# A two-layer transformer on one Trainium2 core: the second attention's products and heads in one block, with 80 maxima beside the products

## The chip, the core and the metric

The kernel runs on one core of a Trainium2 chip. Five engines work side by side, each with its own instruction list, and wait for one another through semaphores: TensorE (PE in the profile; PEld are its weight loads), VectorE (DVE), ScalarE (ACT), GpSimd (POOL) and SyncE (SP), which here only issues DMA transfers. SBUF is the on-chip memory of 128 partitions; PSUM holds TensorE's results in eight banks of 512 float32 per partition. The metric is the time of one execution on the device in microseconds. Three runs of the kernel before took 1679.89, 1681.15 and 1681.57 us: median 1681.15 us.

## The reference, cut to what matters

1024 tokens of 512 features pass four sublayers, each as `x = x + layernorm(f(layernorm(x)))`: a latent attention, a gated feed-forward layer (inner width 1792), a second attention with 32 heads of 16 features, and a linear layer with dequantized weights. The change is about the third:

```
qkv = x @ attn_qkvw + attn_qkvb                  # 1024 x 1536
q, k, v = split into 32 heads of hd = 16
scores = einsum('bhqd,bhkd->bhqk', q, k) * scale
probs = softmax(scores)
ctx = einsum('bhqk,bhkd->bhqd', probs, v)
out = ctx @ attn_ow + attn_ob
```

## The kernel before, in words

Everything is float32 in effect. Where an exact product is wanted, each operand is split into an upper part that TensorE takes at full rate and a lower part (the rest), and three matmuls (upper-upper, upper-lower, lower-upper) are summed.

A block is a piece of program with one instruction list for each engine; the next block begins when all engines have ended the last one. The stages around the change are these:

1. **Norm block `n2`** (`norm_block`). For each of eight token tiles of 128 TensorE makes the feed-forward's down projection (42 matmuls), VectorE and ScalarE normalize it, add it to `x`, normalize again, TensorE transposes the result and ScalarE and VectorE write it as `h_hi` and `h_lo`. The transposes of tile t stand behind the projection of tile t + 1, those of the last tile behind everything.
2. **Inputs block** (`mha_inputs`). SyncE fetches the weights of queries, keys and values (1 MB each); ScalarE and VectorE split each whole (128 x 2048). TensorE then makes 16 products for queries and keys (feature block of 128 by half the tokens) and 8 for values (a token tile each), 12 matmuls each. For queries and keys ScalarE adds the bias into `full`, VectorE casts the upper part and subtracts the lower, and SyncE stores both in DRAM (`qk_scratch`, 256 KB each). Values go to DRAM too (`v_scratch`), 32 columns per head: 16 values and 16 ones, so that mixing also gives the sums of the softmax.
3. **Heads block** (`mha_heads`). Eight groups of four heads. A group's *stacks* hold, on 48 partitions per head, query and key parts one above the other (three rows of 16), so that one matmul gives the exact score; a 49th row holds the negative maximum (queries) or ones (keys). Twelve transfers of 128 KB build the stacks of a group from `qk_scratch`, three stack buffers rotate.
   - *Maxima.* For the softmax's maximum TensorE makes each score tile once (128 queries x 512 keys) into `ah_ring`, three PSUM banks in turn, and VectorE reduces it to one column: 64 per group, 512 in all. After 32 of them VectorE joins and transposes them, and SyncE writes them as row 49 of the query stack.
   - *Units.* A unit is 128 keys by 512 queries for the four heads. TensorE makes two pairs of scores, ScalarE two exponentials over 1024 columns, TensorE mixes them with the values (eight rows of the trace) into `ah_mix`. 16 units per group, 128 in all. After eight units ScalarE copies out the result and SyncE, VectorE and GpSimd divide it by the sums.
   - *Order.* `maxima_before(n, stage)` says how many maxima TensorE has issued before which part of unit n. 56 stand alone before unit 0, then four stand in each unit until all 512 are issued with unit 114; the last 14 units have none.
   - SyncE issues all transfers in one written order: the first three groups' stacks and values ahead, later groups' stacks in two halves of six between the small transfers of each half group.
4. **Tail block** (`mha_tail`). Output projection, norm, linear layer, norm.

## Time and profile before

| | us |
|---|---|
| median of three runs | 1681.15 |
| profiled execution, its own time | 1682.93 |
| its span, first to last instruction | 1680.7 |
| TensorE busy | 1528.2 (91%) |
| VectorE busy | 1039.1 (62%) |
| ScalarE busy | 809.2 (48%) |
| GpSimd busy | 227.9 (14%) |

The profile comes from one execution; its span is 2.2 us shorter than that execution's own time. Rows of the view by windows give, for each stretch, its length and then each engine's busy time with the number of instructions, TensorE's granted clock as a share of full speed (1.00 is 2.4 GHz, 0.50 is 1.2 GHz), the busy share of the 16 DMA engines and what they moved. Rows of the timeline give start, duration, engine, source line, operation, what is written and read, shapes and count, and in brackets how long the engine had been idle and what released it. Rows of a source line give the shortest, middle and longest duration in ns. Records of neighbouring instructions on one engine can overlap, so a pace is read from starts. Busy shares over the whole span say little here: stages with different limits follow one another.

### The profile page before, as it was taken

Reading aid. Unit: us, or ns where it says so; the run is one execution under the profiler, and the core shown is the slowest. Engines: PE = TensorE matmul, PEld = TensorE weight load, DVE = VectorE, ACT = ScalarE, POOL = GpSimd, SP = SyncE. Lnnn points to the kernel's source line nnn. Section 1 sums busy time; section 2 is a strip of 40 time slices with the busy share of each in tenths; the row PEclk is TensorE's granted clock in tenths of the full one; section 3 lists DMA queues with packets and bytes.
Section 4 is the critical chain, followed back from the end, with each engine's and each line's share of the span. In section 5 each row is a group of like instructions: output and inputs, shape, how many; then the busy total and the mean of one; then the engine's idle time right before and its main releaser. Section 6 shows DMA issues by size and latency. Waiting matters only on the chain. (4 is left out here: it accounts for less than half of the span.)

```text
span 1680.7 us, 22663 instructions
## 1 busy us (share of the span) xinstructions
PE 1528.2 (91%) x8286; PEld 1004.9 (60%) x8286; DVE 1039.1 (62%) x1801; ACT 809.2 (48%) x1458; POOL 227.9 (14%) x225
## 2 busy tenths in 40 slices
PE   6867999999999999969989998969599999999987
PEld 4645666666777666748768887848443333333254
DVE  5744666666666666625543443644199999999345
ACT  4325666666666666522122212213017777777834
POOL 2752111111111121000000000000000033331200
PEclk9977999999999999989979999989859999999999
DMA  4142212212221221153211111024670334431001
GB/s 132 55 180 69 88 61 67 66 62 67 94 67 60 67 67 39 32 182 99 88 63 57 61 53 50 1 82 176 170 106 8 76 78 87 88 71 35 18 13 44
DMA packets 71714, 125.23 MB, mean 75 GB/s; under 512 B 13054, under 2 KB 38782, under 8 KB 70318
## 3 DMA queue, kind: packets, MB, share of 16 engines
q1 hardware_dynamic: 71540, 123.67, 25.4%
q8 instruction: 67, 1.10, 0.3%
q14 instruction: 43, 0.35, 0.1%
q0 software_dynamic: 64, 0.11, 0.0%
HBM read 87.23 MB, written 33.85 MB: 72 GB/s over the span
## 5 line engine op out<-in xcount | busy, mean ns | idle before, releaser
L1641 DVE TENSOR_REDUCE ah_minus_half<-ah_ring 128x1 f32<-128x512 f32 x512 | 317.5, 679 | 35.3 <-PE ah_ring L1569 35.3
L958 DVE TENSOR_REDUCE mh_minus_max<-mh_score 128x1 f32<-128x128 f32 (+7 forms) x256 | 193.7, 757 | 196.2 <-PE mh_score L772 196.0
L1624 ACT ACTIVATE ah_probs<-ah_score 128x1024 f32<-128x1024 f32 x256 | 247.8, 1022 | 134.6 <-PE ah_score L1584 134.0
L1569 PE MATMUL ah_ring<-ah_k_stack,ah_q_stack 48*128 48x512 f32 x512 | 203.8, 491 | 34.8 <-DMA ah_k_stack<-qk_scratch 18.9
L1569 PEld LDWEIGHTS ah_ring<-ah_k_stack,ah_q_stack 48*128 48x128 f32 x512 | 92.3, 197 | 210.0 <-DVE ah_minus_half L1641 184.2
L882 ACT ACTIVATE mh_probs<-mh_score,mh_minus_max 128x128 f32<-128x128 f32 (+7 forms) x256 | 189.9, 742 | 35.7 <-DVE mh_minus_max L958 33.3
L1584 PE MATMUL ah_score<-ah_q_stack,ah_k_stack 49*128 49x512 f32 x512 | 154.2, 434 | 1.7 <-ACT ah_probs L1624 1.7
L768 PE MATMUL mh_score<-shared,h_hi 128*128 128x512 f32 (+3 forms) x384 | 151.6, 395 | 2.7 <-ACT mh_probs L882 2.7
L1031 POOL TENSOR_TENSOR h_lo<-mh_pe,h_hi 64x512 fp32r<-64x512 f32 x64 | 81.8, 1278 | 470.0 <-ACT h_hi L868 466.4
L1599 PE MATMUL ah_mix<-ah_probs,ah_v 128*32 128x512 f32 x1024 | 137.2, 608 | 0.6 <-ACT ah_probs L1624 0.6
L769 PE MATMUL mh_score<-shared,h_hi 128*128 128x512 f32 (+3 forms) x384 | 131.9, 344 | 0.0
L770 PE MATMUL mh_score<-shared,h_lo 128*128 128x512 f32 (+3 forms) x384 | 131.8, 343 | 0.0
L782 PE MATMUL mh_turn<-ident,mh_probs 128*128 128x128 f32 x672 | 107.5, 277 | 2.5 <-DVE mh_high_turned L967 0.4
L768 PEld LDWEIGHTS mh_score<-shared,h_hi 128*128 128x128 f32 x384 | 73.1, 190 | 60.0 <-ACT mh_probs L882 36.5
L892 ACT COPY mh_high_turned<-mh_turn 128x128 f32<-128x128 f32 (+3 forms) x128 | 54.6, 426 | 105.0 <-PE mh_turn L787 105.0
L808 PE MATMUL mh_mix<-mh_high_turned,ck 128*64 128x512 f32 (+3 forms) x512 | 102.8, 524 | 0.0
L967 DVE COPY mh_high_turned<-mh_turn 128x512 f32<-128x512 f32 x128 | 87.5, 684 | 4.6 <-PE mh_turn L782 3.4
L1584 PEld LDWEIGHTS ah_score<-ah_q_stack,ah_k_stack 49*128 49x128 f32 x512 | 79.6, 187 | 17.9 <-ACT ah_probs L1624 15.3
L787 PE MATMUL mh_turn<-ident,mh_probs 128*128 128x128 f32 x480 | 84.4, 274 | 0.0
L1204 DVE TENSOR_TENSOR d<-x,ff_up 128x512 f32<-128x512 f32 x28 | 19.3, 688 | 102.7 <-PE ff_up L1157 102.7
L1178 ACT ACTIVATE x<-ff_gate 128x512 f32<-128x512 f32 x28 | 16.7, 598 | 136.8 <-PE ff_gate L1157 136.8
L770 PEld LDWEIGHTS mh_score<-shared,h_lo 128*128 128x128 f32 x384 | 73.0, 190 | 7.0
(224 smaller groups left out, 2892.9 us busy)
## 6 DMA issues: line engine op xcount, KB each, us to landing
mh_w<-in_w_pairs SPq DMA_DIRECT2D x16, 896.0 KB, 5.6
x<-in_w_inner SPq DMA_DIRECT2D x14, 768.0 KB, 4.1
pe_scratch<-fr_pe_out SPq DMA_DIRECT2D x4, 2048.0 KB, 6.6
mh_pe<-pe_scratch SPq DMA_DIRECT2D x16, 512.0 KB, 4.0
mh_spread<-inverse_scratch SPq DMA_DIRECT2D x64, 128.0 KB, 2.9
a_scratch<-mh_mixed SPq DMA_DIRECT2D x32, 256.0 KB, 2.3
x<-a_scratch SPq DMA_DIRECT2D x8, 1024.0 KB, 5.7
qk_scratch<-shared SPq DMA_DIRECT2D x32, 256.0 KB, 2.0
```

The costliest lines, as they stand in the source:

```text
L768: nc.tensor.matmul(out, q_hi[:, i % 2, e, q], m["kt_hi"][e][:, k], start=True, stop=False)
L769: nc.tensor.matmul(out, q_hi[:, i % 2, e, q], m["kt_lo"][e][:, k], start=False, stop=False)
L770: last = nc.tensor.matmul(out, q_lo[:, i % 2, e, q], m["kt_hi"][e][:, k], start=False, stop=not diagonal)
L782: last = nc.tensor.transpose(turn_ps[0][:, j, :], probs[:, s % 2, j * P:(j + 1) * P], ident[:])
L808: last = nc.tensor.matmul(mix_ps[e * CR:(e + 1) * CR, q0:BANK], m["ck"][:, j, 0:CR], high_turned[:, j, e, q0:BANK], start=j == 0, stop=j = ...
L882: nc.scalar.activation(probs[:, s % 2, 0:width], score_ps[s % 2][:, base:base + width], ACT.Exp, bias=minus_max[:, s % 4:s % 4 + 1], accum ...
L958: nc.vector.reduce_max(minus_max[:, s % 4:s % 4 + 1], score_ps[s % 2][:, base:base + width], AX.X, negate=True).then_inc(max_ready, 1)
L1569: return nc.tensor.matmul(ring[:, m % 3, :], q_stack[a][stack_rows(p, PARTS), c, t * P:(t + 1) * P], k_stack[a][stack_rows(p, PARTS), c, h ...
L1584: last = nc.tensor.matmul(score_ps[c][:, p, :], k_stack[a][rows, c, j * P:(j + 1) * P], q_stack[a][rows, c, half * BANK:(half + 1) * BANK] ...
L1599: last = nc.tensor.matmul(mix_ps[rows, :], v[a][:, j, rows], probs[:, 2 * (u % 2) + c, p * BANK:(p + 1) * BANK], start=j == 0, stop=j == N ...
L1624: nc.scalar.activation(probs[:, 2 * (u % 2) + c, :], score_ps[c][:].rearrange("p e n -> p (e n)"), ACT.Exp, scale=MHA_SCALE).then_inc(prob ...
L1641: nc.vector.reduce_max(minus_half[:, m:m + 1], ring[:, m % 3, :], AX.X, negate=True).then_inc(max_taken, 1)
```

## The change

The inputs block is gone. A class `Products` holds its work, spread over the two blocks beside it:

- In the norm block SyncE fetches the weights when the operand `d`, on whose place they go, has been split. ScalarE and VectorE split the first two pieces (128 columns of the key and of the query weights) while tile 6 is in work; TensorE makes products 0 and 1, which need only the first half of the tokens, between the last projection and the last transposes.
- In the heads block products 2 to 23 come first. Their order is now key and query of the same feature block in turn, so that groups 0 and 1 can be loaded after products 0 to 3. Their PSUM banks are those of the scores. From product 8 on there are five maxima beside each product, two behind its first six matmuls and three behind the rest: 80 before unit 0. The other 432 are spread over units 0 to 113, 3.79 per unit.
- ScalarE writes the upper part straight from PSUM, VectorE the lower part straight from PSUM with one instruction; the weights are split in pieces of 128 x 512.
- Values stay in SBUF (eight tensors, ones written by GpSimd); `v_scratch` and its transfers go.
- Group 0's stacks are issued half by SyncE, half by ScalarE; groups 1 and 2 by SyncE beside the stores; groups 3 to 7 by ScalarE, one transfer behind the second exponential of units 1 to 12 of a group.
- Many tensors of the later stages lie at fixed places inside `d`, `down_hi`, `down_lo`, `shared` and `h`.

The diff, cut to its core:

```diff
+                if following is not None:
+                    following.load(sp)
...
+            if following is not None:
+                pe.wait_ge(ht_used, NT // 2)
+                for n in range(2):
+                    following.product(pe, n, range(ND))
...
+                if following is not None and t == NT - 2:
+                    following.upper(act, 0)
+                    following.upper(act, 1)
...
-def mha_inputs(nc, io, h, spare, w_hi, w_lo, hi, lo, scratch):
...
+    def piece(self, i):
+        if i < 2 * ND:
+            c, cols = 1 - i % 2, slice(i // 2 * P, (i // 2 + 1) * P)
+            return tuple(m[c][:, :, cols] for m in (self.w, self.w_hi, self.w_lo))
+        return tuple(m[2][:, i - 2 * ND, :] for m in (self.w, self.w_hi, self.w_lo))
...
+    def product(self, pe, n, steps):
+        if steps[0] == 0:
+            wait(pe, self.lo_ready, min(n - 3, self.NQK))
+            wait(pe, self.v_ready, n - 3 - self.NQK)
+            pe.wait_ge(self.w_ready, n // 4 * 2 + 1 + n % 2 if n < self.NQK else 2 * ND + ND)
...
+    def take_upper(self, act, n):
+        kind, blk, _ = self.place(n)
+        if n == 0:
+            act.wait_ge(self.bias_in, 32)
+        act.wait_ge(self.ready, n + 1)
+        if n >= 4:
+            act.wait_ge(self.part_out[n % 4], 32 * (n // 4))
+        row = kind * ND + blk
+        self.nc.scalar.activation(self.ring[:, n % 4, 0, :], self.bank(n), ACT.Identity, bias=self.bias_qk[:, row:row + 1]
+                                  ).then_inc(self.hi_ready, 1)
...
+    def take_lower(self, dve, n):
+        kind, blk, _ = self.place(n)
+        row = kind * ND + blk
+        dve.wait_ge(self.hi_ready, n + 1)
+        self.nc.vector.scalar_tensor_tensor(self.ring[:, n % 4, 1, :], self.bank(n), self.bias_qk[:, row:row + 1],
+                                            self.ring[:, n % 4, 0, :].bitcast(F32), ALU.add, ALU.subtract).then_inc(self.lo_ready, 1)
...
-        PER_UNIT = NMAX // NUNIT
-        LEAD = 6 * PER_UNIT
-        FIRST = HALF_MAX + LEAD
+        FROM = 8
+        FIRST = 5 * (products.COUNT - FROM)
+        AHEAD = 6
...
+        def maxima_at(unit):
+
+            return min(FIRST - (-unit * (TOTAL - FIRST) // (UNITS - NT - AHEAD)), TOTAL)
...
+        def maxima_beside(n, part):
+
+            return max(5 * (n - FROM) + (2, 5)[part], 0)
...
-            def load_stacks(g, row_halves):
-                a = g % DEPTH
-                wait(sp, scores_ready, 2 * NUNIT * (g - DEPTH + 1))
...
-            def load_v(g):
-                a = g % DEPTH
-                wait(sp, mixed, NUNIT * (g - DEPTH + 1))
-                sp.dma_start(v[a][:], v_rows[:, :, 4 * g * 2 * HD:4 * (g + 1) * 2 * HD]).then_inc(v_in[a], 16)
...
-                load(g)
+            for n in range(4):
+                products.store(sp, n, scratch["qk"])
+            for n in range(4):
+                sp.wait_ge(products.part_out[n], 32)
+            load_stacks(sp, 0, (0,))
+            for n in range(4, products.NQK):
+                products.store(sp, n, scratch["qk"])
+                if n in (5, 7):
+                    load_stacks(sp, 1, (n // 2 - 2,))
             put_max(0, 0)
+            for n in range(4):
+                sp.wait_ge(products.part_out[n], 32 * products.NQK // 4)
             put_ones(2)
-            load(2)
+            load_stacks(sp, 2, range(2))
             put_max(0, 1)
             sp.dma_start(bias_f[:], io["biases"]).then_inc(later_in, 16)
...
-                if DEPTH <= g + 2 < GROUPS:
-                    load_stacks(g + 2, (0,))
...
+                if (g, u, c) == (0, 0, 0):
+                    pe.wait_ge(products.v_ready, NT)
...
+            for n in range(2, products.COUNT):
+                for part in range(2):
+                    products.product(pe, n, range(2 * part, 2 * part + 2))
+                    while done < maxima_beside(n, part):
+                        one_maximum(done)
+                        done += 1
...
+            pieces = {1: (2, 3), 3: (4, 5), 7: (6, 7), 8: (8,), 9: (9,), 10: (10,), 11: (11,)}
+            for n in range(products.NQK):
+                products.take_upper(act, n)
+                for i in pieces.get(n, ()):
+                    products.upper(act, i)
+                if n == 3:
+                    for i in range(4):
+                        act.wait_ge(products.part_out[i], 32)
+                    load_stacks(act, 0, (1,))
...
+            def load_one(g, n):
+                a = g % DEPTH
+                if n == 0:
+                    act.wait_ge(scores_ready, 2 * NUNIT * (g - DEPTH + 1))
+                p, kind, n, part = stack_loads[n]
+                stack = (q_stack, k_stack)[kind][a]
+                act.dma_start(stack[64 * p + n * HD:64 * p + (n + 1) * HD, :, :].bitcast(F32),
+                              qk_rows[part, kind, g, p]).then_inc(stacks_in[a], 16)
...
+                    if 1 <= u <= STACK_DMAS and DEPTH <= g + 2 < GROUPS:
+                        load_one(g + 2, u - 1)
...
+            for n in range(products.COUNT + 1):
+                if n < products.NQK:
+                    products.take_lower(dve, n)
+                elif n < products.COUNT:
+                    take_value(n)
+                for i in pieces.get(n, ()):
+                    products.lower(dve, i)
+                until = maxima_beside(n + 1, 1) if n + 1 < products.COUNT else FIRST if n < products.COUNT else TOTAL
+                while m < until:
...
+                    if inverted < NHALF * GROUPS and maxima_at(NT * (inverted + 1) + AHEAD) < min(m + 1, TOTAL):
+                        shares.invert(dve, inverted)
```

Where instructions move, the order of the instruction lists shows it. The first place is TensorE at the end of the norm block. Before: `n_py` is the down projection, `n_pt` the transposes, `ai_ps` the first product.

```order
L1900 MATMUL n_py<-down_lo,shared 128x512
L1900 MATMUL n_py<-down_hi,shared 128x512
L126 MATMUL n_pt<-ident,n_hn 128x128 x8
L87 UNCONDITIONAL_BRANCH
L1265 UNCONDITIONAL_BRANCH
L1281 MATMUL ai_ps<-h_hi,down_hi 128x512
L1281 MATMUL ai_ps<-h_lo,down_hi 128x512
```

Now (`ah_score` holds the products, `ai_w` are the weights' parts; the 24 matmuls of two products are cut to their first and last):

```order
L1963 MATMUL n_py<-down_lo,shared 128x512
L1963 MATMUL n_py<-down_hi,shared 128x512
L128 MATMUL n_pt<-ident,n_hn 128x128 x4
L1309 MATMUL ah_score<-h_hi,ai_w_hi_11230 128x512
L1309 MATMUL ah_score<-h_lo,ai_w_hi_11230 128x512
...
L1309 MATMUL ah_score<-h_hi,ai_w_lo_11232 128x512
L128 MATMUL n_pt<-ident,n_hn 128x128 x4
L87 UNCONDITIONAL_BRANCH
L1572 UNCONDITIONAL_BRANCH
L1309 MATMUL ah_score<-h_hi,ai_w_hi_11230 128x512
```

The last four transposes stand behind two products, and the third product follows the one block border that is left.

The second place is VectorE from the last products to the maxima. Before: `shared` is the lower part of a query or key product, `d` a value product, `ah_minus_half` a reduced maximum, `ah_rows` the turned maxima.

```order
L1318 TENSOR_TENSOR shared<-d,shared 128x512
L1325 TENSOR_TENSOR d<-ai_ps,ai_bias_v 128x32x16 x8
L1225 UNCONDITIONAL_BRANCH
L1637 UNCONDITIONAL_BRANCH
L1663 MEMSET ah_minus_max 128x32 x2
L1641 TENSOR_REDUCE ah_minus_half<-ah_ring 128x1 x34
L1650 TENSOR_TENSOR ah_minus_max<-ah_minus_half 128x4x2x2
L1641 TENSOR_REDUCE ah_minus_half<-ah_ring 128x1
L1659 STREAM_TRANSPOSE ah_rows<-ah_minus_max 32x32 x4
```

Now, from product 9 on:

```order
L1294 TENSOR_TENSOR ai_w_lo_11234<-ai_w_11228,ai_w_hi_11231 128x512
L1683 TENSOR_REDUCE ah_minus_half<-ah_ring 128x1 x5
L1328 SCALAR_TENSOR_TENSOR ai_ring<-ah_score,ai_bias_qk,ai_ring 128x512
L1294 TENSOR_TENSOR ai_w_lo_11234<-ai_w_11228,ai_w_hi_11231 128x512
L1683 TENSOR_REDUCE ah_minus_half<-ah_ring 128x1 x5
...
L1328 SCALAR_TENSOR_TENSOR ai_ring<-ah_score,ai_bias_qk,ai_ring 128x512
L1683 TENSOR_REDUCE ah_minus_half<-ah_ring 128x1 x4
L1692 TENSOR_TENSOR ah_minus_max<-ah_minus_half 128x4x2x2
```

The reductions stand five by five between the lower parts of the products (and, up to product 11, a piece of weights), instead of in one run behind all of them.

The third place is ScalarE around the units. Before: `ah_probs` are exponentials, `ah_out` the copied result.

```order
L1298 ACTIVATE d<-ai_ps,ai_bias_qk 128x512 x13
L1225 UNCONDITIONAL_BRANCH
L1614 UNCONDITIONAL_BRANCH
L1624 ACT_TABLE_LOAD
L1624 ACTIVATE ah_probs<-ah_score 128x1024 x18
L1619 COPY ah_out<-ah_mix 128x512
```

Now, from the last products to the first units of group 1:

```order
L1321 ACTIVATE ai_ring<-ah_score,ai_bias_qk 128x512 x4
L1643 ACT_TABLE_LOAD
L1643 ACTIVATE ah_probs<-ah_score 128x1024 x18
L1638 COPY ah_out<-ah_mix 128x512
L1643 ACTIVATE ah_probs<-ah_score 128x1024 x16
L1638 COPY ah_out<-ah_mix 128x512
L1643 ACTIVATE ah_probs<-ah_score 128x1024 x2
L1664 DMA ah_q_stack_11958<-qk_scratch 16x2x1024
L1643 ACTIVATE ah_probs<-ah_score 128x1024 x2
L1664 DMA ah_q_stack_11958<-qk_scratch 16x2x1024
```

From group 1 on, a transfer of the stacks stands behind each pair of exponentials, twelve times in a group's sixteen units.

## Rows read from the trace of the kernel before

**Rows 1.** Windows: length, engines' busy us (x instructions), PEclk, DMA share, GB/s.

```profile
1114.40:1122.10 7.70, 1.54 (x8) 0.91 (x6) 5.42 (x11) 1.69 (x4) 0.00 (x0) 0.83 0.00 0
1122.10:1132.20 10.10, 0.01 (x1) 0.01 (x1) 3.26 (x3) 1.90 (x1) 0.00 (x0) 0.50 0.85 299
1132.20:1199.80 67.60, 67.59 (x288) 55.47 (x288) 27.17 (x41) 14.64 (x18) 0.00 (x0) 0.97 0.48 184
1199.80:1218.60 18.80, 0.00 (x0) 0.00 (x0) 0.82 (x3) 1.28 (x1) 0.20 (x1) 0.63 0.83 133
1218.60:1252.10 33.50, 32.57 (x55) 15.28 (x55) 32.59 (x59) 0.00 (x0) 0.00 (x0) 0.50 0.65 98
1252.10:1569.70 317.60, 302.53 (x1822) 115.34 (x1821) 296.59 (x542) 229.50 (x243) 69.36 (x69) 0.99 0.32 63
1569.70:1598.70 29.00, 26.69 (x173) 7.20 (x172) 1.87 (x8) 26.84 (x29) 6.32 (x6) 1.00 0.07 18
1598.70:1680.70 82.00, 63.02 (x244) 44.37 (x240) 44.28 (x122) 31.27 (x58) 3.17 (x3) 0.91 0.08 30
```

**Rows 2.** Timeline: start, us, engine, line, operation, operands, [idle before <- releaser].

```profile
1100.41 2.03 DVE L1893 TENSOR_TENSOR shared<-d,shared 128x1792 fp32r<-128x1792 f32 x1 [0.84 <-ACT shared L1889]
1119.62 1.12 PE L126 MATMUL n_pt<-ident,n_hn 128*128 128x128 f32 x4 [4.79 <-DVE n_hn L204]
1132.19 0.80 PE L1281 MATMUL ai_ps<-h_hi,down_hi 128*128 128x512 f32 x1 [11.46 <-DVE down_lo L1305]
1193.06 0.39 PE L1281 MATMUL ai_ps<-down_hi,h_lo 128*128 128x512 f32 x1
...
1199.40 0.39 PE L1281 MATMUL ai_ps<-down_lo,h_hi 128*128 128x512 f32 x1
1218.64 1.22 PE L1569 MATMUL ah_ring<-ah_k_stack,ah_q_stack 48*128 48x512 f32 x3 [18.85 <-DMA ah_k_stack<-qk_scratch]
```

**Rows 3.** Windows, while the first stacks are fetched.

```profile
1206.00:1218.00 12.00, 0.00 (x0) 0.00 (x0) 0.00 (x0) 0.00 (x0) 0.00 (x0) 0.50 1.05 127
```

**Rows 4.** Timeline of TensorE, two units, one with a join.

```profile
1352.28 0.49 PE L1569 MATMUL ah_ring<-ah_k_stack,ah_q_stack 48*128 48x512 f32 x1 [0.57 <-DVE ah_minus_half L1641]
1352.70 1.06 PE L1599 MATMUL ah_mix<-ah_probs,ah_v 128*32 128x512 f32 x8
1353.70 0.50 PE L1569 MATMUL ah_ring<-ah_k_stack,ah_q_stack 48*128 48x512 f32 x1
...
1355.40 1.06 PE L1599 MATMUL ah_mix<-ah_probs,ah_v 128*32 128x512 f32 x8
```

**Rows 5.** Timeline of VectorE (lone maxima) and of ScalarE (a unit).

```profile
1219.47 20.42 DVE L1641 TENSOR_REDUCE ah_minus_half<-ah_ring 128x1 f32<-128x512 f32 x34 [15.30 <-PE ah_ring L1569]
...
1357.16 1.94 ACT L1624 ACTIVATE ah_probs<-ah_score 128x1024 f32<-128x1024 f32 x2 [0.76 <-PE ah_score L1584]
```

**Rows 6.** Groups by line: busy us, mean ns of one, idle before.

```profile
L1641 DVE TENSOR_REDUCE ah_minus_half<-ah_ring 128x1 f32<-128x512 f32 x512 | 317.5, 679 | 35.3 <-PE ah_ring L1569 35.3
L1318 DVE TENSOR_TENSOR shared<-d,shared 128x512 fp32r<-128x512 f32 x16 | 11.1, 693 | 0.6
L1298 ACT ACTIVATE d<-ai_ps,ai_bias_qk 128x512 f32<-128x512 f32 x16 | 11.0, 690 | 34.3 <-PE ai_ps L1281 34.3
L1325 DVE TENSOR_TENSOR d<-ai_ps,ai_bias_v 128x512 f32<-128x512 f32 x8 | 5.5, 692 | 15.0 <-PE ai_ps L1281 15.0
L943 DVE SCALAR_TENSOR_TENSOR w_vo_lo<-mh_prep,kw,w_vo_hi 128x512 fp32r<-128x512 f32 x16 | 11.9, 743 | 3.7 <-ACT w_vo_hi L856 3.7
```

**Rows 7.** SyncE's issues: timeline, source line (ns), stores' landing, issues by operand.

```profile
1204.19 1.34 SPq L1451 DMA_DIRECT2D ah_q_stack<-qk_scratch  x3
L1451 SPq DMA_DIRECT2D ah_q_stack<-qk_scratch x48: 321/424/1082, 1204.2 to 1509.9; - x48
DMA to landing us min/median/max: 2.0/2.0/3.7
mh_spread<-inverse_scratch SPq DMA_DIRECT2D x64, 128.0 KB, 2.9
```

298 lines of the change are left out of this document (146 added, 152 removed).

## The prediction, made before the changed kernel had run

> **What bounds the kernel now.** I read the span in stretches first [rows 1]. It ends in one line of stages, each of which waits for the one before, so a stretch in which no engine works at its limit is paid in full. From the end of the second norm block to the last mixing product there are seven: 7.7 us in which TensorE works 1.5, 10.1 us without any (0.01), 67.6 us of query, key and value products with TensorE at 67.59, 18.8 us without any, 33.5 us of maxima alone, 317.6 us of units with maxima, and 29.0 us of the last 14 units.
>
> The timeline of TensorE says what ends the gaps [rows 2]: the last transposes wait 4.79 us for VectorE's normed tile, the first product 11.46 us for the split weights, the first maximum 18.85 us for the stacks. With full clock a product matmul comes every (1199.40 - 1193.06)/28 = 0.2264 us, so 288 take 65.2 us; the stretch lasted 67.6 because the clock was low in its first 4 us. The clock column [rows 1] shows 0.83 in the norm's last stretch, with its pause of nearly 5 us, 0.50 in the gap before the products, 0.50 again while the stacks are fetched and in the whole stretch of lone maxima.
>
> In a unit [rows 4] mixing takes 1353.70 - 1352.70 = 1.00 us and four maxima and four scores 1355.40 - 1353.70 = 1.70 us, 0.2125 each: 2.70 us, TensorE without a pause. Once every eight units VectorE joins and turns its maxima, and TensorE waits 0.57 us for a free slot of the ring of three; that unit takes 0.50 us more. 114 x 2.70 + 14 x 0.50 = 314.8 of 317.6 us; the other 2.8 us are the first two units, begun at low clock. VectorE takes 34 reductions in 20.42 us, 0.60 apart (one is recorded with 0.68 [rows 6], so they overlap), and ScalarE's two exponentials take 1.94 us of a unit [rows 5].
>
> **Part 1: weights and two products inside the norm block.** The weights are fetched as soon as the operand `d` is split, and split in ScalarE's and VectorE's pauses. The first two products, 24 x 0.2264 = 5.4 us, stand in the 4.79 us pause, so the last transposes come some 0.6 us later, but at full clock (they took 1.12 us at low). The block therefore ends where it did, at 1122.1 to 1122.3, and product 2 begins at about 1122.7. The other 22 products take 22 x 2.717 = 59.8 us. Without maxima they would end at 1182.5 instead of 1199.8.
>
> **Part 2: stacks and maxima beside the products.** Maxima begin in the middle of product 8, at 1122.7 + 6 x 2.72 + 1.36 = 1140.4 if the stacks are there. They are not: product 3 ends at 1128.4, its two parts (0.69 on ScalarE, 0.74 on VectorE [rows 6]) at 1129.9, and its store, issued in 0.3 us, lands 2.0 us later (2.0 to 3.7 [rows 7]), so 1132.1. Before, the twelve transfers of the first group took from 1204.19 [rows 7] to 1218.64 [rows 2] = 14.4 us. I take the same: 1146.5, a pause of 6 us on TensorE. Bounds: 9 us if twelve ran with nothing beside them and overlapped their start (1141), 20 us if the eight stores and six more transfers behind them take their share of the engines first (1152). I choose 14.4 because the DMA share was already 1.05 in those 12 us at 127 GB/s [rows 3]: the transfers themselves were the limit, not their issue.
> The Trainium skill, "DMA: Bandwidth & Descriptors", "Issuing engines are not separate DMA queues", says that transfers started by several engines share the same 16 DMA engines and that only issue time is saved. By that rule half of the stacks on ScalarE's queue gains nothing over 14.4 us; if the two queues added up, the stacks would land near 1139.5 and the sum would be 5 us better. The row of share 1.05 sides with the rule.
>
> From the first maximum on VectorE is the later one: 80 reductions x 0.60 = 48.1; 8 lower parts of queries and keys by a form that reads PSUM, a bias and the upper part, 0.74 each by the same form elsewhere plus 0.03 between instructions = 6.2; 8 values x 0.72 = 5.8; 4 pieces of value weights x 0.72 = 2.9; two joins with their transposes 2.0. That is 65.0 us, against 15.5 x 2.72 + 80 x 0.213 = 59.2 on TensorE. With a ring of three the two can't run far apart; I add 2.3 us for the handovers (the last value waits for its product) and get the first score at 1146.5 + 67.3 = 1213.8. Before it was 1252.1: **-38.3 us**. If the lower part takes 0.69, as the plain subtraction does [rows 6], that is 0.4 us less. The pause of 6 us will let the clock fall for some us, as nearly 5 us did in the norm, but VectorE is the limit behind it, so I price that at nothing; with TensorE as the limit it is 2.4 us, as in the product stretch (67.6 - 65.2).
>
> Hidden at no cost: the removed stores and loads of values, the cast on VectorE, GpSimd's eight memsets (it is idle there [rows 1]), the later load of the exponential's table, which falls into ScalarE's wait for the last value.
>
> **Part 3: the units.** 432 maxima over the same 114 units instead of 456: 24 x 0.2125 = 5.1 us less. A join moves in front of the units (-0.5) and the first units run at full clock (-2.8). **-8.4 us**. VectorE's load falls with the maxima, so nothing takes their place; in units with three maxima TensorE needs 2.49 us and ScalarE 1.94.
>
> **Part 4: later stacks issued by ScalarE.** Sixty units now have one transfer behind their second exponential. Its issue took 0.42 us on SyncE in the middle of 96, from 0.31 to 1.08 [rows 7]. ScalarE has 2.65 - 1.94 = 0.71 us to spare in a mean unit, so up to about 0.7 us is free: I take 0.42 and no cost; the upper bound 1.08 costs 60 x 0.37 = 22 us; the lower, nothing. No row shows an issue on ScalarE. What does come late: group 3's first maximum is number 192, in unit 29, and its last transfer is issued behind the exponentials of unit 28, 2.0 us after unit 28's first score is done, and lands 2.9 us later (128 KB from DRAM, issue to landing [rows 7]), 4.9. TensorE reaches that maximum at 2.70 + 4 x 0.2125 = 3.6: **+1.3 us** once, 0.4 if it lands in 2.0 like a store, 3.1 if the engines are busy and it takes 4.7. Later groups have more room, as the maxima run ahead less.
>
> What is queued behind the new waits: SyncE's stores of products 4 to 7 stand behind six transfers of group 0 and twelve of group 1. ScalarE writes ring slot n mod 4 only when the store of product n - 4 has landed, and VectorE's maxima stand behind that. By 127 GB/s group 0 and the first half of group 1 are done near 1153, store 6 by 1154; product 10 ends at 1157. Room of 3 us.
>
> **The sum.** -38.3 - 8.4 + 1.3 = -45.4 us. The 29.0 us of the last units (1.94 us of exponentials in 2.07) and the 82.0 us behind [rows 1] stay. Span 1680.7 - 45.4 = 1635.3; the profiled execution, 2.2 us more than its span (1682.93), would be 1637.5; the median of the runs, 1681.15, is 1.8 under it and becomes 1635.7. I say 1636.
>
> **Rivals.**
> ScalarE's issue is dear. Against it: 0.42 median; for it: it stands in line between exponentials, and no row shows it there. At 1.08 each: 1636 + 22 = 1658.
> Stores and stacks collide. 6 MB (24 stack transfers of 128 KB, 12 stores of 256 KB) want the DMA engines within 30 us, at a share of 1.05 for the stacks alone. If the stacks land at 1152 and one slot of the ring waits 4 us: 1646.
> The first stacks are early. ScalarE and SyncE issue in parallel, nothing else moves at first; at 1141 it is 5.5 us less: 1631.
> Slower than before: the same 60 issues, if each holds ScalarE for more than 0.7 + 45/60 = 1.45 us, since the exponentials then set the unit. At 1.6 us they cost 60 x 0.89 = 53 us: 1689. For it: only that a transfer on a busy queue may hold its issuer (1.08 at most on SyncE, with 12 in a row). Against it: it is one transfer per unit, 128 KB in 2.7 us, where the engines move that in 1.0.
> The change doing less than it says: if the products waited for the weights inside the norm, it would show before the last transposes. In the norm's last stretch the DMA share is 0.00 [rows 1], so the fetch finds free engines; it can start when the operand's last split ends, at 1102.4 [rows 2], its first 512 KB are needed on ScalarE at about 1109 and at 299 GB/s take 1.7 us. It gets no number of its own.
>
> **Chances.** Forecast 0.65 (its own range 1630 to 1643); collision 0.14; early stacks 0.09; dear issue 0.08; slower 0.04. The range 1627 to 1653 holds the first three and leaves out most of the last two. About 0.2% (3.4 us) can be told apart by measurement: faster 0.95, within it 0.01, slower 0.04.
>
> **What will show it.** Right: no 11 us wait before the first product; a wait of about 6 us on the stacks' transfers in the middle of product 8, maxima from 1146 on; first exponential near 1214; product cadence 4.4 to 4.5 us for products 8 to 11, then 3.85; units of 2.70 and, every fifth or so, 2.49; ScalarE's issues near 0.42 and no wait of scores for exponentials beyond before's. One wait of 1 to 2 us at unit 29. Wrong: units over 2.7 us where a transfer is issued; VectorE idle in the product stretch while ScalarE waits for a store.

## The result and the profile after

The changed kernel takes 1636.05 us, the median of four runs (1633.25 to 1639.19); before, beside it, 1680.52 us (1679.36 to 1681.57). The ratio is 0.9736, with a 95% interval of 0.9713 to 0.9759. Predicted were 1636 us. One execution, the profiled one of (4) with 1677.60 us, lies more than 1.5% above the fastest of its kernel and is left out of the medians and ratios.

The profiled execution is the shortest of the four: 1633.25 us, span 1631.4, so it lies 2.8 us under the median. The columns are those of [rows 1].

```profile
1114.40:1120.80 6.40, 4.75 (x23) 3.73 (x23) 4.36 (x8) 0.88 (x2) 0.03 (x1) 1.00 0.00 0
1120.80:1143.90 23.10, 17.96 (x78) 14.55 (x78) 9.45 (x16) 8.26 (x14) 4.40 (x9) 0.95 0.80 182
1143.90:1216.70 72.80, 70.34 (x266) 41.89 (x266) 63.48 (x110) 8.81 (x13) 0.39 (x2) 0.97 0.54 124
1216.70:1240.00 23.30, 22.86 (x124) 9.68 (x125) 19.40 (x36) 15.72 (x16) 0.00 (x0) 0.85 0.00 1
1240.00:1549.00 309.00, 297.21 (x1844) 109.91 (x1843) 262.12 (x482) 241.10 (x255) 75.19 (x73) 1.00 0.21 54
1554.40:1631.40 77.00, 62.44 (x240) 44.18 (x240) 44.00 (x122) 30.68 (x57) 3.21 (x3) 0.92 0.08 30
```

The stretches without TensorE (10.1 and 18.8 us) and the lone maxima (33.5 us) of [rows 1] are gone, and the norm's last stretch runs at clock 1.00 instead of 0.83. What answers to [rows 2] in TensorE's timeline:

```profile
1118.55 0.60 PE L128 MATMUL n_pt<-ident,n_hn 128*128 128x128 f32 x4
1120.82 0.47 PE L1309 MATMUL ah_score<-h_hi,ai_w_hi 128*128 128x512 f32 x1 [1.67 <-PEq L87]
...
1143.94 0.79 PE L1580 MATMUL ah_ring<-ah_k_stack,ah_q_stack 48*128 48x512 f32 x2 [5.17 <-DMA ah_k_stack<-qk_scratch]
...
1216.73 0.69 PE L1597 MATMUL ah_score<-ah_q_stack,ah_k_stack 49*128 49x512 f32 x2 [2.34 <-DVE ah_v L1707]
...
1296.65 0.46 PE L1580 MATMUL ah_ring<-ah_k_stack,ah_q_stack 48*128 48x512 f32 x1 [0.78 <-DMA ah_k_stack<-qk_scratch]
```

Before, TensorE waited 4.79, 11.46 and 18.85 us. Now 5.17 us on the first stacks are left, and two waits are new: 2.34 us before the first score and 0.78 us in a unit, on the stacks of group 3. The transfers issued by ScalarE and the stores, by source line (shortest, middle, longest; ns), against [rows 7]:

```profile
L1664 ACTq DMA_DIRECT2D ah_q_stack<-qk_scratch x30: 309/310/314, 1264.6 to 1455.6; - x30
...
L1664 ACTq DMA_DIRECT2D ah_k_stack<-qk_scratch x30: 309/310/330, 1272.1 to 1463.9; - x30
...
L1336 SPq DMA_DIRECT2D qk_scratch<-ai_ring x32: 319/320/640, 1121.9 to 1182.2; - x32
...
DMA to landing us min/median/max: 2.0/3.6/14.8
```

The span, cut at the same events in both traces, beside the terms of the prediction:

| stretch | before | predicted | after |
|---|---|---|---|
| first product of the heads block starts at | - | 1122.7 | 1120.82 |
| from it to the first maximum | - | 23.8 | 23.1 |
| first maximum to first score | - | 67.3 | 72.8 |
| first score at | 1252.1 | 1213.8 | 1216.73 |
| first score to first mixing | 4.9 | 4.9 | 4.4 |
| first to last mixing (127 units) | 340.7 | 333.6 | 327.8 |
| last mixing to the end | 83.0 | 83.0 | 82.5 |
| span | 1680.7 | 1635.3 | 1631.4 |

The total was right; two terms were not, with opposite signs: the stretch from the first maximum to the first score is 5.5 us longer than forecast, the units 5.8 us shorter. The experiments are about these two, about what each part of the change is worth, and about the spread of 6 us between executions.

### The profile page after: what moved, and what is told of

The parts are those of the page before. It is cut to its first block and busy times, and to the rows that moved or that the text cites. A ratio compares the mean times of both kernels' runs of the same rounds, so it can differ in the third digit from the quotient of the medians.

```text
span 1631.4 us, 22633 instructions
## 1 busy us (share of the span) xinstructions
PE 1512.2 (93%) x8286; PEld 990.9 (61%) x8286; DVE 1031.7 (63%) x1792; ACT 810.1 (50%) x1467; POOL 232.1 (14%) x233
## 5 line engine op out<-in xcount | busy, mean ns | idle before, releaser
L1580 PE MATMUL ah_ring<-ah_k_stack,ah_q_stack 48*128 48x512 f32 x512 | 184.3, 461 | 15.3 <-DMA ah_k_stack<-qk_scratch 5.9
L1580 PEld LDWEIGHTS ah_ring<-ah_k_stack,ah_q_stack 48*128 48x128 f32 x512 | 81.5, 187 | 176.2 <-DVE ah_minus_half L1683 160.4
L1597 PEld LDWEIGHTS ah_score<-ah_q_stack,ah_k_stack 49*128 49x128 f32 x512 | 76.0, 187 | 22.4 <-ACT ah_probs L1643 15.5
L1963 PE MATMUL n_py<-down_hi,shared 128*128 128x512 f32 x224 | 72.5, 400 | 4.9 <-DVE shared L1956 4.9
```

What stands on the lines that cost most here:

```text
L1580: return nc.tensor.matmul(ring[:, m % 3, :], q_stack[a][stack_rows(p, PARTS), c, t * P:(t + 1) * P], k_stack[a][stack_rows(p, PARTS), c, h ...
L1597: last = nc.tensor.matmul(score_ps[c][:, p, :], k_stack[a][rows, c, j * P:(j + 1) * P], q_stack[a][rows, c, half * BANK:(half + 1) * BANK] ...
```

## Experiments

Parts of the change were undone or altered one at a time, then the rules found were tested and used. Every ratio is against the kernel before, run on the same chip. The changed kernel itself ran on one chip only; the medians of the kernel before, taken beside each run, lie between 1679.24 and 1680.52 us, so 1.3 us of a difference between medians can be the chip's. "Block start" is the first product of the heads block.

**1. The two parts of the front.** First without maxima beside products, then with part 1 undone.

```diff
 def maxima_beside(n, part):
-    return max(5 * (n - FROM) + (2, 5)[part], 0)
+    return 0
```

> The changed kernel with its 80 first maxima in one run behind the products, as before, instead of five beside each product from product 8 on. In the changed kernel's profile product 2 begins at 1120.8, the first score stands at 1216.7. Main theory (a maximum beside a product costs about 0.31 us, since a product with five takes 4.28 us instead of 2.72, and one alone costs VectorE's 0.60): products end at 1120.8 + 22 x 2.72 = 1180.6, then 80 x 0.60 = 48 and two joins, first score near 1231; the clock falls beside the lone maxima, 2.8 us more in the first units. Time 1636 + 14 + 3 = 1653. Rival (placing them beside the products saves nothing that the pause for the stacks and the switching between product and maximum don't take back): 1636 to 1640.

Measured 1648.68 us (1644.86 to 1653.8), ratio 0.9819 (0.9795 to 0.9843): 12.6 us over the changed kernel. Windows, products and then lone maxima:

```profile
1118.60:1182.80 64.20, 60.64 (x264) 49.33 (x264) 22.61 (x35) 17.14 (x27) 4.41 (x9) 1.00 0.70 181
1182.80:1231.50 48.70, 46.40 (x81) 21.34 (x80) 48.45 (x89) 0.00 (x0) 0.39 (x2) 0.55 0.25 33
```

TensorE no longer waits for the stacks, which land while it makes products, but the 80 maxima then go at VectorE's pace (48.7/80 = 0.61 us each) with TensorE at clock 0.55. From block start to first score it takes 112.9 us against 95.9. Putting maxima beside products is worth 17 us of that stretch in the traces and 12.6 in the medians.

```diff
-        vector_work=vector_work, projected=used, following=products)
+        vector_work=vector_work, projected=used)
 # and in the heads block, ahead of everything:
+            products.load(sp)
...
-            for n in range(2, products.COUNT):
+            for n in range(products.COUNT):
...
+            products.upper(act, 0)
+            products.upper(act, 1)
...
+            products.lower(dve, 0)
+            products.lower(dve, 1)
```

> The changed kernel with the weights' fetch, the first two pieces and products 0 and 1 taken out of the norm block and put at the head of the heads block. Main theory (part 1 of the prediction): the fetch of the first 512 KB and one piece split by ScalarE and VectorE stand in front, 5 to 6 us; two products of 2.72 us more behind it; 2.4 us of low clock. Time 1636 + 13 = 1649, and the pause before the stacks stays as it is (about 5 us). Rival (the products are followed by a pause for the stacks, which counts from product 3, so nothing before it is hidden, but VectorE limits the rest, so low clock costs nothing): 1646. Rival (the norm block's end moved by as much as it gained): 1637.

Measured 1649.05 us (1644.9 to 1651.4), ratio 0.9814 (0.9794 to 0.9835). TensorE's timeline:

```profile
1127.42 0.79 PE L1309 MATMUL ah_score<-h_hi,ai_w_hi 128*128 128x512 f32 x1 [7.17 <-DVE ai_w_lo L1294]
...
1156.13 0.77 PE L1581 MATMUL ah_ring<-ah_k_stack,ah_q_stack 48*128 48x512 f32 x2 [2.99 <-DMA ah_k_stack<-qk_scratch]
```

The wait for the weights is back (7.17 us), and two products more stand behind it. Part 1 is worth 13.0 us, as this run's main theory had it (1649).

**2. Which engine sets the pace: VectorE's reductions made shorter.**

```diff
-nc.vector.reduce_max(minus_half[:, m:m + 1], ring[:, m % 3, :], AX.X, negate=True).then_inc(max_taken, 1)
+nc.vector.reduce_max(minus_half[:, m:m + 1], ring[:, m % 3, 0:256], AX.X, negate=True).then_inc(max_taken, 1)
```

> The changed kernel with each maximum's reduction over the first 256 of its 512 columns only (half of the columns is left out of the maxima). TensorE's work is unchanged; VectorE's 0.60 per maximum becomes about 0.33. Theory of the ring (in a unit with four maxima the fourth waits for the slot of the first, which is free 0.53 + 0.68 + 0.06 = 1.27 us after its matmul began; TensorE is not the limit): units fall from 2.70 to about 2.35, the product stretch by 3 to 4 us, the joins' 0.5 us go; time 1600 to 1606. Theory of the prediction (a unit is TensorE's 2.70 us without a pause): units stay at 2.70, only the joins' waits and the handovers beside the products go, 1628 to 1632.

Measured 1602.14 us (1597.74 to 1603.39), ratio 0.9535 (0.9519 to 0.9551). Two rows of VectorE beside value products of the changed kernel, then of this one:

```profile
1192.85 1.89 DVE L1683 TENSOR_REDUCE ah_minus_half<-ah_ring 128x1 f32<-128x512 f32 x3 [0.61 <-PE ah_ring L1580]
1194.65 0.68 DVE L1707 TENSOR_TENSOR ah_v<-ah_score,ai_bias_v 128x512 f32<-128x512 f32 x1
```

```profile
1187.18 1.09 DVE L1683 TENSOR_REDUCE ah_minus_half<-ah_ring 128x1 f32<-128x256 f32 x3 [1.28 <-PE ah_ring L1580]
1188.19 0.68 DVE L1707 TENSOR_TENSOR ah_v<-ah_score,ai_bias_v 128x512 f32<-128x512 f32 x1
1189.42 0.76 DVE L1683 TENSOR_REDUCE ah_minus_half<-ah_ring 128x1 f32<-128x256 f32 x2 [0.56 <-PE ah_ring L1580]
```

Beside value products the pace did not move: from the first value to the last, seven products, it is 29.88 us in the changed kernel (1186.11 to 1215.99) and 29.87 here (1179.65 to 1209.52), though VectorE is now idle 1.28 + 0.56 us in such a product. There VectorE was not the bound. It was the bound in two other places: products 9 to 12 take 4.25 to 4.29 us instead of 4.43 to 4.51, and product 15, beside which VectorE joins and turns the first maxima, 4.26 instead of 5.05. That is 1.6 of the 3.0 us by which this trace is shorter from first maximum to first score (69.8 against 72.8 us). In the units the pace did move: from first to last mixing it is 299.0 us instead of 327.8. TensorE's weight loads of a unit with four maxima, in the changed kernel and in this one, show why (a row is the load, so its start is the moment TensorE takes the matmul up):

```profile
1239.32 0.18 PEld L1580 LDWEIGHTS ah_ring<-ah_k_stack,ah_q_stack 48*128 48x128 f32 x1 [0.84 <-DVE ah_minus_half L1683]
1239.33 0.29 PEld L1597 LDWEIGHTS ah_score<-ah_q_stack,ah_k_stack 49*128 49x128 f32 x2
1239.43 0.44 PEld L1580 LDWEIGHTS ah_ring<-ah_k_stack,ah_q_stack 48*128 48x128 f32 x2
1239.70 0.39 PEld L1597 LDWEIGHTS ah_score<-ah_q_stack,ah_k_stack 49*128 49x128 f32 x2
1240.60 0.18 PEld L1580 LDWEIGHTS ah_ring<-ah_k_stack,ah_q_stack 48*128 48x128 f32 x1 [0.51 <-DVE ah_minus_half L1683]
1241.03 0.16 PEld L1612 LDWEIGHTS ah_mix<-ah_probs,ah_v 128*32 128x32 f32 x8 [0.25 <-issue]
```

VectorE's row of the same unit, and then the loads of the kernel with half reductions:

```profile
1239.86 2.48 DVE L1683 TENSOR_REDUCE ah_minus_half<-ah_ring 128x1 f32<-128x512 f32 x4 [0.22 <-PE ah_ring L1580]
```

```profile
1354.30 0.18 PEld L1580 LDWEIGHTS ah_ring<-ah_k_stack,ah_q_stack 48*128 48x128 f32 x1 [0.24 <-DVE ah_minus_half L1683]
1354.72 0.16 PEld L1612 LDWEIGHTS ah_mix<-ah_probs,ah_v 128*32 128x32 f32 x8 [0.24 <-issue]
```

The fourth maximum, just ahead of the mixing, needs the slot of the unit's first, 1.28 us earlier (1239.32 to 1240.60): 0.53 from the matmul to its reduction (1239.33 to 1239.86), 0.68 for the reduction, and the rest until TensorE takes up the next. Then 0.43 to the mixing and 1.00 of mixing: 2.71, and 2.70 is the usual unit. With three maxima there is no such wait, and the unit takes 2.12 (1.12 + 1.00). The same wait stands in the units of the kernel before, for instance:

```profile
1354.97 0.18 PEld L1569 LDWEIGHTS ah_ring<-ah_k_stack,ah_q_stack 48*128 48x128 f32 x1 [0.51 <-DVE ah_minus_half L1641]
```

The changed kernel has 24 units of 2.12 us: 24 x (2.70 - 2.12) = 13.9 us, where 12.8 were measured between first and last mixing. With half reductions the wait shrinks by 0.27 us, and units of 2.44 replace those of 2.70. The direct test, a fourth slot in the ring, was not made.

**3. Another placing inside a unit.** The four maxima of a unit stood one behind the last mixing, two between the two score pairs and one before the mixing. Now one stands between the pairs and two before the mixing, so that the wait for the ring falls elsewhere.

```diff
-return (now, min(now + (then - now + 1) // 2, then), min(now + (3 * (then - now) + 2) // 4, then))[stage]
+return (now, min(now + 1, then), min(now + 3, then))[stage]
```

> The changed kernel with the four maxima of a unit placed 1 behind the mixing, 1 between the two pairs of scores and 2 before the mixing, instead of 1, 2 and 1. Ring theory (between two mixings stand four maxima, the fourth waits 1.27 us for the slot of the first wherever they stand, then 0.43 to the mixing's start and 1.00 for it): 2.70 per unit, unchanged, 1636. Rival (a maximum alone before the mixing costs 0.58 because matmuls of the two row halves run in pairs): with two before the mixing the unit is 2.4 to 2.5 and the time near 1615.

Measured 1638.02 us (1634.12 to 1639.19), ratio 0.9746 (0.9729 to 0.9764). Units of 2.70 and 2.13 us stay: the ring theory's 1636, not the rival's 1615. A placing that only moves the wait gains nothing.

**4. How often TensorE changes between products and maxima**: one, one, one and two maxima behind each quarter of a product, in place of two and three behind the halves.

```diff
-    return max(5 * (n - FROM) + (2, 5)[part], 0)
+    return max(5 * (n - FROM) + (1, 2, 3, 5)[part], 0)
-    for part in range(2):
-        products.product(pe, n, range(2 * part, 2 * part + 2))
+    for part in range(4):
+        products.product(pe, n, range(part, part + 1))
```

> The changed kernel with the same five maxima beside each product, but in four places (1, 1, 1 and 2, behind every third matmul) instead of two (2 and 3). Theory of switching (between a product matmul of 128 rows and a maximum of 48 TensorE loses about 0.1 us each way: 0.34 and 0.31 between starts instead of 0.23): two more places cost 0.4 us per product, 15.5 products 6 us: 1642. Theory of VectorE (the product stretch is set by reductions and the ring, TensorE has time to spare): an even spread keeps VectorE busier, its idle 0.57 us per product goes: 1630.

Measured 1654.19 us (1650.08 to 1666.48), ratio 0.9863 (0.9815 to 0.991): 18 us over the changed kernel, where 6 were expected. The direction was right and the size was not. TensorE, changed kernel and then this one, both at clock 1.00:

```profile
1191.76 0.40 PE L1309 MATMUL ah_score<-ai_w_hi,h_lo 128*128 128x512 f32 x1
1192.00 0.39 PE L1309 MATMUL ah_score<-ai_w_lo,h_hi 128*128 128x512 f32 x1
1192.31 0.73 PE L1580 MATMUL ah_ring<-ah_k_stack,ah_q_stack 48*128 48x512 f32 x3
1192.97 0.50 PE L1309 MATMUL ah_score<-ai_w_hi,h_hi 128*128 128x512 f32 x1
1193.31 0.40 PE L1309 MATMUL ah_score<-ai_w_hi,h_lo 128*128 128x512 f32 x1
```

```profile
1240.04 0.50 PE L1309 MATMUL ah_score<-ai_w_hi,h_hi 128*128 128x512 f32 x1
...
1240.61 0.40 PE L1309 MATMUL ah_score<-ai_w_lo,h_hi 128*128 128x512 f32 x1
1240.94 0.49 PE L1580 MATMUL ah_ring<-ah_k_stack,ah_q_stack 48*128 48x512 f32 x1
1241.36 0.50 PE L1309 MATMUL ah_score<-ai_w_hi,h_hi 128*128 128x512 f32 x1
```

Between product matmuls it is 0.235 us; the last one before a group of maxima takes 0.31 to 0.33, the first one behind it 0.34: 0.19 us per group. A group of one or two maxima takes 0.42, one of three 0.65. That makes 12 x 0.235 + 0.42 + 0.65 + 2 x 0.19 = 4.27 us for a product with five maxima, measured 29.88/7 = 4.27, and 12 x 0.235 + 4 x 0.42 + 4 x 0.19 = 5.26 with four groups, measured 5.29 (from value to value on VectorE: 1229.46, 1234.75, 1240.04). The two more changes cost the 0.4 us that was expected; what the expectation left out is that five maxima take 1.07 us in two groups and 1.68 in four. The Trainium skill, "TensorEngine Tiling (Array Packing)", "Key Properties", says that changing the tiling mode, not just the tile, drains TensorE. These rows agree in so far as going from 128 rows to 48 and back costs 0.19 us; what of it is the drain they don't show.

**5. Fewer maxima beside products**: ten fewer, and then from product 10 on, but six beside each.

```diff
-        FROM = 8
+        FROM = 10
```

> The changed kernel with maxima beside products from product 10 on instead of 8: 70 stand before unit 0, 442 in the units. The stacks landed at 1143.9, which is when product 10's first half ends (1120.8 + 8 x 2.72 + 1.36), so the pause of 5.2 us and the low clock behind it (to 1148) go. Ring theory: first score 9 to 11 us earlier; ten more maxima in units cost 0.58 each where they turn a unit of three into one of four, 3.3 to 5.8 us; net -5: 1631. Theory of the prediction (a maximum in a unit costs 0.21, VectorE limits the product stretch): first score 9 earlier, units 2.1 dearer, net -7: 1629. If the pause is what makes executions differ by 5 us (1633 or 1639), this kernel's runs lie closer together.

Measured 1633.43 us (1630.7 to 1639.07), ratio 0.9731 (0.9707 to 0.9754). No wait for the stacks is left in its trace; the first score stands 89.2 us behind block start against 95.9, and the units take 332.1 us against 327.8. One expectation failed outright: without the pause for the stacks the executions should have come closer together, and they lie 8.4 us apart, the changed kernel's 5.9. And here the collision of the prediction's rivals shows. ScalarE waits for a store to land before it may write a slot of the ring, VectorE's lower part and its reductions come late behind it, and TensorE waits for a slot of the maxima:

```profile
1142.85 0.69 ACT L1321 ACTIVATE ai_ring<-ah_score,ai_bias_qk 128x512 fp32r<-128x512 f32 x1 [4.54 <-DMA qk_scratch<-ai_ring]
```

```profile
1146.86 1.14 PE L1580 MATMUL ah_ring<-ah_k_stack,ah_q_stack 48*128 48x512 f32 x2 [1.07 <-DVE ah_minus_half L1683]
```

Products 10 and 11 take 6.1 and 6.6 us, with that wait and low clock behind it, where they take 4.5 each in the changed kernel. These 3.7 us are of the size of what is missing: the first score came 6.7 us earlier, and 9 to 11 were expected.

```diff
-        FROM = 8
-        FIRST = 5 * (products.COUNT - FROM)
+        FROM = 10
+        FIRST = 6 * (products.COUNT - FROM)
...
-            return max(5 * (n - FROM) + (2, 5)[part], 0)
+            return max(6 * (n - FROM) + (3, 6)[part], 0)
```

> The changed kernel with maxima beside products from product 10 on, six each (3 and 3): 84 before unit 0, 428 in the units. Against the kernel with 70 from product 10 on (1633.4): 14 more beside products, by VectorE's 6 x 0.60 + 0.71 = 4.3 us and TensorE's 2.72 + 6 x 0.21 + 0.4 = 4.4 us per product about 0.2 each, 3 us; 14 fewer in units, 0.58 each by the ring theory, 8 us less. Ring theory: 1629. Theory of the prediction (0.21 per maximum in a unit): 1633 to 1634.

Measured 1639.0 us (1631.19 to 1639.23), ratio 0.9741 (0.9713 to 0.9769). This is a miss for both theories (1629, and 1633 to 1634): in its trace the first score stands 97.3 us behind block start, not the 3 us more than 89.2 that were expected. TensorE waits 2.26 us there for a slot of the maxima, and ScalarE waits for stores here too (10.6 us in two gaps). Neither kernel can be told from the changed one. A maximum costs (95.9 - 89.2)/10 = 0.67 us at most beside the products, the stacks' pause included, and (332.1 - 327.8)/10 = 0.43 in the units, so moving a few changes little.

**6. Who issues the stacks.** First the later groups from SyncE again, in two halves of six.

```diff
-                    if 1 <= u <= STACK_DMAS and DEPTH <= g + 2 < GROUPS:
-                        load_one(g + 2, u - 1)
 # SyncE, in its written order:
+                if DEPTH <= g + 2 < GROUPS:
+                    wait(sp, scores_ready, 2 * NUNIT * g)
+                    load_stacks(sp, g + 2, (0,))
...
+                if DEPTH <= g + 2 < GROUPS:
+                    load_stacks(sp, g + 2, (1,))
```

> The changed kernel with the stacks of groups 3 to 7 issued by SyncE in two halves of six, at the places where the kernel before had them, and none by ScalarE. In the changed kernel an issue took ScalarE 0.31 us behind its second exponential and no score waited for it; one maximum waited 0.78 us for the last transfer of group 3. Main theory (the move to ScalarE is worth nothing either way in the units): 1635 to 1637, no wait for a stack at unit 29, small transfers of the divided results up to 3 us later without anyone waiting. Rival (SyncE's halves hold back the turned maxima, row 49, so that a first score of a half group waits): 1640 or more, with a wait on rows.

Measured 1639.53 us (1637.05 to 1646.82), ratio 0.9766 (0.974 to 0.9793); the interval overlaps the changed kernel's. Neither theory was right: the first had 1635 to 1637 and no wait for a stack, the second a wait for row 49. The trace has one long wait for a stack, where the changed kernel has a short one (0.78 us, above), and a stretch of low clock behind it:

```profile
1298.01 0.76 PE L1585 MATMUL ah_ring<-ah_k_stack,ah_q_stack 48*128 48x512 f32 x1 [3.28 <-DMA ah_k_stack<-qk_scratch]
```

```profile
1297.00:1310.00 13.00, 11.99 (x47) 4.67 (x48) 6.81 (x16) 3.88 (x4) 2.14 (x3) 0.50 0.10 36
```

The wait of 3.28 us and four units at clock 0.50 (6.17, 4.16, 4.16, 3.89 us between mixings) cost 6.3 us against the same four of the changed kernel (3.37, 2.71, 3.30, 2.70). No cost of ScalarE's issues shows: the usual units take 2.70 and 2.12 us in both traces. Then group 0's stacks from SyncE alone:

```diff
-                if n == 3:
-                    ...
-                    load_stacks(act, 0, (1,))
-            load_stacks(sp, 0, (0,))
+            load_stacks(sp, 0, range(2))
```

> All twelve transfers of group 0's stacks issued by SyncE, none by ScalarE. If the transfers themselves are the limit (the prediction's choice): first maximum within 0.7 us of the changed kernel's against the block's first product (23.1 us), median 1636 to 1637. If the second issuer adds speed: 12 x 0.44 us of issue one behind the other, the first maximum 2.6 us later or more, median 1638 to 1641.

```profile
1139.78 0.79 PE L1580 MATMUL ah_ring<-ah_k_stack,ah_q_stack 48*128 48x512 f32 x2 [5.74 <-DMA ah_k_stack<-qk_scratch]
```

Block start was 1116.08, so the first maximum stands 23.7 us behind it. In the changed kernel's trace it is 23.1 us, but in the six other traces with the same front it is 20.4 to 22.9: one program's transfers land 2.7 us apart from trace to trace. One trace of this kernel can't decide between the 0.7 us of the main theory and the 2.6 of the rival. The median, 1640.42 us (1634.29 to 1641.34), ratio 0.9758 (0.9739 to 0.9778), fell on the rival's side, with an interval that overlaps the changed kernel's. What the second issuer is worth stays open.

**7. The spread of the executions, and TensorE's clock behind two pauses.** The traces of kernels with the same front show the clock fall after the pause for the stacks and after the pause before the first score, and come back at different times. Windows of 23.3 us from about the first score: the placing of (3), four units ahead (8), the last value early (this section), and the version with three edits (8).

```profile
1218.20:1241.50 23.30, 23.18 (x108) 10.24 (x109) 16.91 (x32) 13.57 (x14) 0.00 (x0) 0.65 0.00 1
```

```profile
1216.90:1240.20 23.30, 22.75 (x98) 9.33 (x102) 15.55 (x30) 12.97 (x14) 0.00 (x0) 0.63 0.00 1
```

```profile
1216.10:1239.40 23.30, 22.17 (x121) 8.46 (x117) 21.03 (x39) 15.75 (x16) 0.00 (x0) 0.93 0.00 1
```

```profile
1206.20:1229.50 23.30, 21.66 (x117) 9.11 (x118) 20.47 (x37) 15.07 (x16) 0.40 (x2) 0.85 0.01 1
```

A mean of 0.85 (the changed kernel, above) is 0.15/0.5 x 23.3 = 7 us at 1.2 GHz, 0.65 is 16 us, 0.93 is 3 us. In the trace of (3) the units 0 to 7 take 25.3 us against 22.0 in the changed kernel's, and from the first maximum to the first score it is 74.9 us against 72.8. These 5.4 us make up the difference of the two spans (1637.3 and 1631.4) with 1.2 us in the tail and -0.6 ahead of the first maximum. The changed kernel's own four executions go the same way: spans of 1631.4, 1631.9, 1636.3 and 1637.3 us have a mean granted clock of 0.966, 0.966, 0.962 and 0.961. The next run takes the second pause away: VectorE takes the last value ahead of the last three maxima, and each pair of the first scores waits only for the values whose banks it takes.

```diff
-                if (g, u, c) == (0, 0, 0):
-                    pe.wait_ge(products.v_ready, NT)
+                if (g, u) == (0, 0):
+                    pe.wait_ge(products.v_ready, NT - 2 + 2 * c)
...
 # VectorE: behind value 22 only the maxima that stand before product 23's second half
```

> VectorE takes the last value before the last three maxima of the product stretch, and the first pair of scores waits for the values whose banks it takes, not for all eight. Main theory (the 2.34 us pause before the first score is on the path, and the low clock behind it costs more and varies between executions): first score 2.3 us earlier against the last product, no clock under 0.9 in the 12 us behind it, about 3.5 us more from that: median near 1630 us, and executions closer together than the 1633 to 1639 of the changed kernel. Rival (the pause matters alone, the clock falls anyway): 1633.5 to 1634.

```profile
1215.41 0.40 PE L1309 MATMUL ah_score<-ai_w_lo,h_hi 128*128 128x512 f32 x1
1215.74 0.73 PE L1580 MATMUL ah_ring<-ah_k_stack,ah_q_stack 48*128 48x512 f32 x3
1216.08 0.62 PE L1597 MATMUL ah_score<-ah_q_stack,ah_k_stack 49*128 49x512 f32 x2
```

Measured 1629.65 us (1628.28 to 1633.89), ratio 0.9706 (0.9689 to 0.9723). The first score stands 0.67 us behind the last product matmul instead of 3.39, the first mixing 5.84 instead of 7.79, and the clock is low for 3 us instead of 7 to 16. The median is 6.4 us under the changed kernel's, with intervals that overlap by a little. Against the last kernel of (6) and the first of (8), which ran on the same chip and keep both pauses but have an edit of their own, they don't overlap. The earlier mixing is 2.0 us of it. The trace does not show the rest: from block start to last mixing it has 427.6 us, the changed kernel's 428.1, since it took 1.6 us more from the first maximum to the last product matmul (71.0 against 69.4, with clock 0.51 over its first 8.6 us); its execution, 1633.89 us, is the slowest of the four. So a cause in the clock for the other 4.4 us is argued, not shown.

What makes the executions of one kernel differ is not explained by the two pauses either. The executions of this kernel still lie 5.6 us apart. Those of the first kernel of (5), which has no pause for the stacks, lie 8.4 us apart, and those of the three-edit version of (8), which has neither pause (but waits for slots of up to 1.2 us, as in (5)), 10.4 us. In that last one, too, the longest span goes with the lowest clock (1635.3 us at 0.961; 1624.9 at 0.969), and its traced execution was at 1.2 GHz for 7 us behind the first score, as the changed kernel's was. The clock also fell where TensorE had hardly paused: for 3.5 us at 1147.7 behind a wait of 1.07 us in the first kernel of (5),

```profile
1147.70:1151.20 3.50, 3.50 (x9) 2.11 (x8) 1.50 (x3) 0.46 (x1) 0.00 (x0) 0.51 1.09 338
```

and for 3 us at 1221 in this one, where the longest wait of the 5 us before was 0.49 us. The time goes with the clock; what takes the clock down is only in part the two pauses.

**8. Maxima four units ahead instead of six**, and a version with three edits.

```diff
-        AHEAD = 6
+        AHEAD = 4
```

> The maxima run four units ahead instead of six, so the same 432 stand in 116 units instead of 114. Ring theory (a fourth maximum in a unit makes it 2.70 us instead of 2.12, a unit without maxima is 2.07): six units of 2.70 fewer, eight of 2.12 more, two of 2.07 fewer: -3.4 us, median near 1632.6. The prediction's reading (each maximum costs 0.21 us of TensorE wherever it stands): -0.4 us, 1635.6.

Measured 1640.62 us (1634.96 to 1643.34), ratio 0.9763 (0.9743 to 0.9783). A miss: 4.6 us over the changed kernel instead of 3.4 under. The units 5 to 126 took 312.2 us against 313.3 in the changed kernel, so a third of the gain that the ring theory forecast is there; the first five took 19.2 against 14.5, at the low clock of the second row in (7). The second version joins this edit to the last value early (7) and to maxima from product 10 on (5):

> Three edits together: the last value ahead of the last maxima, maxima beside products from product 10 on (70 instead of 80), four units ahead. If they add up: 1636 - 6 - 2.5 - 3.4 = about 1624 us. If the clock falls anyway behind the first score: 1627 to 1628.

Measured 1628.32 us (1626.8 to 1637.21), ratio 0.9709 (0.9684 to 0.9733): 7.7 us under the changed kernel in the median (the intervals overlap by 0.002), and not to be told from (7) alone. The three edits did not add up to the 1624 us expected; it is the other theory's 1627 to 1628, and the clock did fall behind the first score, as that theory had it (0.85, in (7)).

## Why the prediction was right, and where it was not

- *Part 1* right: no wait for weights, the last transposes at full clock, 0.60 us instead of 1.12. Product 2 came 1.9 us before the forecast. In the traces with this front it starts anywhere from 1116.1 to 1121.6, behind a program that is the same, so these 1.9 us say nothing about the change. Worth 13.0 us, by (1).
- *The stacks* right: the pause was 5.2 us, forecast 6, at a DMA share of 1.02 (1132 to 1144), which fits the transfers as the limit. The rule of the Trainium skill, "DMA: Bandwidth & Descriptors", "Issuing engines are not separate DMA queues", was the prediction's choice here. The trace agrees as far as it goes: two queues that add up would have halved the 14.4 us and left TensorE no pause, and the pause was there. (The prediction put that case at 5 us less; by its own terms, a first maximum at 1140.4 at the earliest instead of 1146.5, it is 6.1.) Whether the second issuer is worth some 2 us is open (6).
- *The product stretch* wrong in size: "From the first maximum on VectorE is the later one" failed. 67.3 us were forecast, 72.8 came. Up to product 12 the pace was 4.4 to 4.5 us, and there VectorE did set it, by 0.2 us (2); from there on it was 4.25 to 4.30 instead of 3.85, but for 5.05 in product 15 with VectorE's join. The failed term is TensorE's, 15.5 x 2.72 + 80 x 0.213: it added two paces that were each read in a run of like matmuls, and left out 0.19 us per change between them and the groups' own length (4). By (4), (4.27 - 3.85) x 12 products = 5.0 of the 5.5 us; the low clock is a likely rest, not measured by itself. VectorE's own terms were right: the lower part took 0.742 us, 0.74 forecast from [rows 6].
- *The clock behind the pause* was priced at nothing because VectorE was taken for the limit. This stretch takes 2 us more in the trace of (3) than in the changed kernel's (7), with the clock low for longer. The pause before the first score was in the sum (2.3 us); that the clock would fall again behind it was not.
- *The units* wrong in size: -7.1 forecast, -12.8 measured. The failed step is the reading of [rows 4], "TensorE without a pause", 0.2125 us a maximum. The matmul rows overlap and are grouped over the wait; the weight loads show 0.51 us of it (2). A unit with three maxima takes 2.12, not 2.49. The saving at full clock for the first units (-2.8) came by half a us only: the first took 3.86 us, 3.79 before, and the second 2.70, 3.32 before.
- *ScalarE's issues* right and cheaper than assumed, 0.31 us each; the dear issue (1.08 us) and the slower case (over 1.45 us) did not come, the longest of the sixty took 0.33. Group 3's wait was 0.78, forecast 1.3.
- *Collision* did not occur as a cost, although a store took up to 14.8 us to land. ScalarE, which would have waited for a slot of the ring, waited for products. Only its gap of 5.3 us, marked "issue", is another: 2.5 us until the stores of products 0 to 3 had landed, as the program wants it before the first stacks, and then its own six issues. The pause for the stacks hid the collision: in the traces without that pause it is there, with waits of TensorE of 1.07 and 2.26 us (5), and of 2.12 and 1.40 us in the kernel with lone maxima (1), where ScalarE waits for stores in eight gaps, 19.2 us. ScalarE's row in the changed kernel:

```profile
L1321 ACT ACTIVATE ai_ring<-ah_score,ai_bias_qk 128x512 fp32r<-128x512 f32 x16 | 10.7, 688 | 43.9 <-PE ah_score L1309 37.5 <-issue 5.3 <-PEq L87 1.1
```

So the gain and the main waits were right by their mechanisms, but that 1636 was met to the microsecond is luck: 5.5 us too little and 5.8 us too much cancelled, and the median lies 2.8 us above the profiled execution, which itself was 4.2 us under its forecast of 1637.5.
